# Side rows dealt out by a plan, a third row buffer, and ScalarE fetching in all edge passes of a graph network kernel

## The reference, cut to what matters

```python
h = relu(layernorm(x)); x = x + L0(h)      # typed attention, softmax over each node's incoming edges
h = relu(layernorm(x)); x = x + L1(h)      # gated attention: softmax sum, maximum and mean over edges
h = relu(layernorm(x)); x = x + L2(h)      # polynomial of edge weights, summed per node
h = relu(layernorm(x)); x = x + L3(h)      # three convolutions:
def conv(h, W, b):
    m = concatenate([h[dst], h[src], edge_attr], axis=1) @ W + b
    return segment_sum(m, dst, num_segments=n_nodes)
```

## Time and profile before

| | us |
|---|---|
| profiled execution, time | 11757.73 |
| its span | 11755.6 |
| median of three runs | 11757.57 |
| POOL busy | 8127.3 (69%) |
| VectorE busy | 4012.2 (34%) |
| ScalarE busy | 3490.3 (30%) |
| TensorE busy | 1335.8 (11%) |

### The profile page before, as it was taken

How to read it: one execution, slowest core, us unless ns; L and a number is a source line. 1 busy time by engine, 2 the same in 40 slices (tenths; PEclk the granted TensorE clock), 3 DMA queues, 4 the chain that set the end, 5 groups by cost and what they waited for, 6 DMA issues and landing times. The chain is left out here.

```text
span 11755.6 us, 88443 instructions
## 1 busy us (share of the span) xinstructions
PE 1335.8 (11%) x6735; PEld 1000.0 (9%) x6735; DVE 4012.2 (34%) x5478; ACT 3490.3 (30%) x4561; POOL 8127.3 (69%) x8534
## 2 busy tenths in 40 slices
PE   6100000030000000496111000200000010000001
PEld 4100000020000000374000000200000010000001
DVE  3365555645555555696111111111111101111111
ACT  3333333312222222375333222223222212332221
POOL 5777777677777776401777777677777767777776
PEclk8555555555555555798555555555555555555555
DMA  9333333323333333000222222222222212222222
GB/s 348 129 112 108 108 108 111 105 39 102 110 110 107 113 107 81 13 1 23 67 65 66 65 68 62 62 51 56 53 56 56 53 50 51 56 53 56 56 53 50
DMA packets 448676, 922.38 MB, mean 78 GB/s; under 512 B 211206, under 2 KB 241837, under 8 KB 432952
## 3 DMA queue, kind: packets, MB, share of 16 engines
q0 software_dynamic: 272736, 378.88, 14.7%
q1 hardware_dynamic: 157672, 535.74, 12.5%
q10 hardware_dynamic: 17648, 2.29, 0.1%
HBM read 456.45 MB, written 459.77 MB: 78 GB/s over the span
## 5 line engine op out<-in xcount | busy, mean ns | idle before, releaser
L912 POOL DMA_INDIRECT arena<-tab,src x6087 | 5746.2, 944 | 2631.0 <-issue 1890.5
L2334 DVE TENSOR_TENSOR_SCAN arena<-cv_keep,arena 128x768 f32<-128x768 f32 (+1 forms) x476 | 751.9, 1627 | 5040.6 <-ACT arena L2190 5040.6
L912 POOL DMA_INDIRECT arena<-tab,spread x1539 | 1453.1, 944 | 469.3 <-issue 469.0
L2179 ACT COPY cv_keep<-keep 128x736 f32<-128x736 f32 x204 | 166.0, 814 | 2707.6 <-issue 2707.6
L2195 ACT COPY arena<-arena 128x1472 f32<-128x1472 f32 (+1 forms) x204 | 588.2, 2883 | 551.6 <-DVE arena L2334 551.6
L2190 ACT COPY arena<-arena 128x1472 f32<-128x1472 f32 x204 | 545.2, 2673 | 666.4 <-DMA arena<-tab,src 430.0
L1147 PE MATMUL e_t<-ident,arena 128*68 128x128 f32 (+1 forms) x2 | 0.8, 396 | 4037.2 <-PEq L1492 2046.4
L2258 PE MATMUL cv_t<-ident,arena 128*81 128x128 f32 (+1 forms) x294 | 137.9, 469 | 2616.8 <-ACT arena L2202 1722.9
L1147 PEld LDWEIGHTS e_t<-ident,arena 128*68 128x68 f32 (+1 forms) x2 | 0.3, 132 | 4037.6 <-issue 4037.6
L2272 PE MATMUL cv_t<-ident,arena 128*64 128x128 f32 (+1 forms) x3 | 1.3, 426 | 2975.7 <-ACT arena L2195 2975.7
L1835 PE MATMUL po_u<-arena,Hn 128*128 128x448 bf16 x1564 | 300.9, 354 | 279.9 <-DVE Hn L1942 279.9
(11 more groups left out here) (373 smaller groups left out, 6810.2 us busy)
## 6 DMA issues: line engine op xcount, KB each, us to landing
arena<-tab SPq DMA_DIRECT2D x11520, 0.2 KB
arena<-tab ACTq DMA_DIRECT2D x6912, 0.2 KB
rows<-arena SPq DMA_DIRECT2D x68, 1506.5 KB, 5.6
rows3b<-arena SPq DMA_DIRECT2D x136, 736.0 KB
arena<-tab,src POOLq DMA_INDIRECT x6087
rows<-arena SPq DMA_DIRECT2D x68, 920.0 KB
rows<-arena SPq DMA_DIRECT2D x68, 828.0 KB, 4.5
arena<-tab SPq DMA_DIRECT2D x3200, 0.5 KB
```

What stands on the lines that cost most here:

```text
L912: pool.indirect_dma_start(out=rows[b][:, j, :], out_offset=None, in_=table, in_offset=bass.IndirectOffsetOnAxis(ap=idx[:, at:at + 1].bitca ...
L2334: ins = v.tensor_tensor_scan(out=part, data0=keep[:, 0:(f1 - f0) * C1], data1=part, initial=0.0, op0=ALU.mult, op1=ALU.add)
```

## The change

A function `rows_plan` deals the pieces of all side columns to the iterations of the loop over blocks, evenly: a piece goes to iteration i at the latest where its block is i - closes, at the earliest where it is i - opens, and in between by its share of all pieces. SP and ScalarE each have their plan in every pass; ScalarE's part (pieces 5 to 7) comes at the end of its loop body, for block c + 2. Each piece waits for its buffer on its own. Attention and gated attention have side columns in 3 of 4 blocks, the second and third convolution in 13 of 16; the convolutions have three row buffers.

```diff
-ATT_SHARE = (2, 5)
-CONV_SHARE = (3, 4)
-SP_ROWS = 80
+ATT_SHARE = (3, 4)
+GATED_SHARE = (3, 4)
+CONV_SHARE = ((3, 4), (13, 16), (13, 16))
+SP_EDGE = 80
+SP_CONV = 80
+def rows_plan(share, first, stop, opens, closes):
+    jobs = [(c, k) for c in range(LISTED) if aided(c, share) for k in range(first // LOADS, stop // LOADS)]
+    plan = [[] for _ in range(NC)]
+    at = 0
+    for i in range(NC):
+        while at < len(jobs) and (jobs[at][0] + closes <= i or
+                                  jobs[at][0] + opens <= i and at * LISTED < (i + 1) * len(jobs)):
+            plan[i].append(jobs[at])
+            at += 1
+    return plan
...
@@ attention_edges_phase
+        of_sp = rows_plan(ATT_SHARE, 0, SP_EDGE, -1, 0)
+        of_act = rows_plan(ATT_SHARE, SP_EDGE, P, -3, -2)
...
-                for later in (0, 1):
-                    if aided(c + later, ATT_SHARE):
-                        wait(sp, s_wtd, c + later - 2)
-                        chunks = range(0, P // LOADS // 2) if later else range(P // LOADS // 2 if c else 0, P // LOADS)
-                        fetch_rows(nc, sp, mybir.EngineType.SP, g.lists[:, 0, :], g.tab0, c + later, chunks,
-                                   kvr[(c + later) % 3], s_side[side_of(c + later, ATT_SHARE)[0]])
+                for x, k in of_sp[c]:
+                    wait(sp, s_wtd, x - 2)
+                    side_rows(sp, mybir.EngineType.SP, x, k)
...
                 nc.scalar.copy(out[:, :, 0:D].rearrange("p j f -> p f j"), mix[:, :, 1:C1]).then_inc(s_copied, 1)
+                for x, k in of_act[c]:
+                    wait(act, s_wtd, x - 2)
+                    side_rows(act, mybir.EngineType.Activation, x, k)
...
@@ gated_edges_phase
+        of_sp = rows_plan(GATED_SHARE, 0, SP_EDGE, -2, -1)
+        of_act = rows_plan(GATED_SHARE, SP_EDGE, P, -3, -2)
...
                 nc.scalar.copy(out[:, :, 0:D].rearrange("p j f -> p f j"), mix[:, :, 1:C1]).then_inc(s_copied, 1)
+                for x, k in of_act[c]:
+                    wait(act, s_wtd, x - 2)
+                    side_rows(act, mybir.EngineType.Activation, x, k)
...
@@ conv_layer
-    for b in range(2):
+    for b in range(3):
         rin[b], at = view(g, at, C, D)
...
+        of_sp = rows_plan(share, 0, SP_CONV, -3, -2)
+        of_act = rows_plan(share, SP_CONV, P, -3, -2)
+        def side_rows(eng, engine, c, k):
+            wait(eng, s_in, c - 2)
+            fetch_rows(nc, eng, engine, g.lists[:, 2, :], g.tab3, c, range(k, k + 1), rin[c % 3],
+                       s_side[side_of(c, share)[0]])
...
             for c in range(NC):
-                wait(sp, s_in, c + 1)
-                if k == 0 and c + 2 < NC:
+                wait(sp, s_in, c + 1 if c else 0)
+                if k == 0 and c + 2 < NC and c:
                     load_attrs(c + 2)
-                side_rows(sp, mybir.EngineType.SP, c + 2, early)
+                half = (len(of_sp[c]) + 1) // 2 if c else len(of_sp[c])
+                for x, part in of_sp[c][:half]:
+                    side_rows(sp, mybir.EngineType.SP, x, part)
...
                 wait(sp, s_copied, c + 1)
                 sp.dma_start(dest[:, c * C:c * C + C, :], rows).then_inc(s_st, 16)
-                side_rows(sp, mybir.EngineType.SP, c + 2, late)
+                for x, part in of_sp[c][half:]:
+                    side_rows(sp, mybir.EngineType.SP, x, part)
...
                 give(c)
-                if len(of_act):
-                    act.wait_ge(s_in, c + 1)
-                    side_rows(act, mybir.EngineType.Activation, c + 2, of_act)
+                if c:
+                    for x, part in of_act[c]:
+                        side_rows(act, mybir.EngineType.Activation, x, part)
```

More of the change, by code:

```diff
@@ L960, in attention_edges_phase @@
         works = work[:, :].rearrange("p (f j) -> p f j", j=C1)
+        of_sp = rows_plan(ATT_SHARE, 0, SP_EDGE, -1, 0)
+        of_act = rows_plan(ATT_SHARE, SP_EDGE, P, -3, -2)
+        def side_rows(eng, engine, c, k):
+            fetch_rows(nc, eng, engine, g.lists[:, 0, :], g.tab0, c, range(k, k + 1), kvr[c % 3],
+                       s_side[side_of(c, ATT_SHARE)[0]])
         @block.gpsimd
@@ L1496, in gated_edges_phase, with side_rows @@
         pre, prob = few[:, 0, :], few[:, 1, :]
+        of_sp = rows_plan(GATED_SHARE, 0, SP_EDGE, -2, -1)
+        of_act = rows_plan(GATED_SHARE, SP_EDGE, P, -3, -2)
+        def side_rows(eng, engine, c, k):
+            fetch_rows(nc, eng, engine, g.lists[:, 1, :], g.tab1, c, range(k, k + 1), rin[c % 3],
+                       s_side[side_of(c, GATED_SHARE)[0]])
         @block.gpsimd
@@ L1502, in _ @@
                 .then_inc(s_first, 16)
-            gather_columns(pool, g.tab1, g.src, rin, s_gath, s_wtd, ATT_SHARE)
+            gather_columns(pool, g.tab1, g.src, rin, s_gath, s_wtd, GATED_SHARE)
         @block.sync
@@ L1565, in _ @@
                 dve.wait_ge(s_flags, c + 1)
-                dve.wait_ge(s_gath[c % 3], gathered(c, ATT_SHARE, 3))
-                if aided(c, ATT_SHARE):
-                    slot, full = side_of(c, ATT_SHARE)
+                dve.wait_ge(s_gath[c % 3], gathered(c, GATED_SHARE, 3))
+                if aided(c, GATED_SHARE):
+                    slot, full = side_of(c, GATED_SHARE)
                     dve.wait_ge(s_side[slot], full)
@@ L2051, in conv_layer @@
     s_ea = [sem(f"attrs{b}") for b in range(2)]
-    s_gath = [pool_sem(g, f"gathered{b}") for b in range(2)]
+    s_gath = [pool_sem(g, f"gathered{b}") for b in range(3)]
     s_side = [sem(f"side{n}") for n in range(4)]
+    share = CONV_SHARE[k]
     s_row = pool_sem(g, "fixed_rows")
@@ L2064, in conv_layer @@
     at = 0
-    rin, ea, hd = ([None] * 2 for _ in range(3))
-    for b in range(2):
+    rin = [None] * 3
+    ea, hd = ([None] * 2 for _ in range(2))
+    for b in range(3):
         rin[b], at = view(g, at, C, D)
@@ L2094, in conv_layer, with side_rows @@
         block = inner.enter_context(nc.Block())
[L2096 to L2100, removed]
+        of_sp = rows_plan(share, 0, SP_CONV, -3, -2)
+        of_act = rows_plan(share, SP_CONV, P, -3, -2)
+        def side_rows(eng, engine, c, k):
+            wait(eng, s_in, c - 2)
+            fetch_rows(nc, eng, engine, g.lists[:, 2, :], g.tab3, c, range(k, k + 1), rin[c % 3],
+                       s_side[side_of(c, share)[0]])
         @block.gpsimd
         def _(pool):
-            gather_columns(pool, g.tab3, g.src, rin, s_gath, s_in, CONV_SHARE)
+            gather_columns(pool, g.tab3, g.src, rin, s_gath, s_in, share)
             fix = bass.IndirectOffsetOnAxis(ap=g.fix[:, 0:1].bitcast(U32), axis=0)
@@ L2138, in _ @@
                     load_attrs(c)
-            early, late = range(0, SP_ROWS // LOADS // 2), range(SP_ROWS // LOADS // 2, SP_ROWS // LOADS)
-            for c in range(2):
-                side_rows(sp, mybir.EngineType.SP, c, range(0, SP_ROWS // LOADS))
             for c in range(NC):
-                wait(sp, s_in, c + 1)
-                if k == 0 and c + 2 < NC:
+                wait(sp, s_in, c + 1 if c else 0)
+                if k == 0 and c + 2 < NC and c:
                     load_attrs(c + 2)
-                side_rows(sp, mybir.EngineType.SP, c + 2, early)
+                half = (len(of_sp[c]) + 1) // 2 if c else len(of_sp[c])
+                for x, part in of_sp[c][:half]:
+                    side_rows(sp, mybir.EngineType.SP, x, part)
+                if k == 0 and not c:
+                    wait(sp, s_in, 1)
+                    load_attrs(2)
                 wait(sp, s_copied, c + 1)
                 sp.dma_start(dest[:, c * C:c * C + C, :], rows).then_inc(s_st, 16)
-                side_rows(sp, mybir.EngineType.SP, c + 2, late)
+                for x, part in of_sp[c][half:]:
+                    side_rows(sp, mybir.EngineType.SP, x, part)
             n_out = 0
@@ L2182, in take @@
                     act.wait_ge(s_chained, c)
-                act.wait_ge(s_gath[b], gathered(c, CONV_SHARE, 2))
-                if aided(c, CONV_SHARE):
-                    slot, full = side_of(c, CONV_SHARE)
+                act.wait_ge(s_gath[c % 3], gathered(c, share, 3))
+                if aided(c, share):
+                    slot, full = side_of(c, share)
                     act.wait_ge(s_side[slot], full)
@@ L2189, in take @@
                     nc.scalar.copy(chain[:, D:R3, 1:C1], ea[b].rearrange("p j f -> p f j"))
-                nc.scalar.copy(chain[:, 0:D, 1:C1], rin[b].rearrange("p j f -> p f j")).then_inc(s_in, 1)
+                nc.scalar.copy(chain[:, 0:D, 1:C1], rin[c % 3].rearrange("p j f -> p f j")).then_inc(s_in, 1)
             def give(c):
@@ L2214, in copy_z @@
                 nc.scalar.copy(z[:, t, :], ps_o[b][:, 0:D]).then_inc(s_z, 1)
-            of_act = range(SP_ROWS // LOADS, P // LOADS)
             scale(0)
-            for c in range(2):
-                side_rows(act, mybir.EngineType.Activation, c, of_act)
+            for x, part in of_act[0]:
```

(1 more changed line is left out.)

## The result

The changed kernel takes 12370.68 us (median of 4 runs, 12369.15 to 12383.37) against 11758.11 us for the kernel before (4 runs): ratio 1.052, 95% interval 1.0502 to 1.0538. The forecast was 12,390 (12,280 to 12,500). The profiled execution took 12383.37 us, its span is 12381.6, which is 626 us more than before.

What follows compares the result with a forecast made beforehand. POOL's gathers bound the passes, a buffer besides in the first convolution. Attention +84, gated +557, first convolution -47, second and third together +36 make +630 us on 11757.73: 12,390 us, range 12,280 to 12,500.

Steps and rivals of the forecast that it cites:

- Gathers as the bound: All five edge passes of the kernel before: bound by POOL's number of gathers, 1.25 us each.
- the gated chain: Gated pass: fetch, mask and VectorE's work follow serially, so a block with a fetch takes 41.9 us against POOL's 27.5.
- The price of a fetch: ScalarE's loop end: 18.8 us idle after a 2.8 us copy, 19.0 us more than without a fetch.
- the gated term: Gated pass, first gather to last result copy: 2499 us against 1942.0 before, +557.
- that term: Attention, first gather to last exponentials: ScalarE's chain becomes the limit, 2015 us against 1930.9 before, +84.
- rival B: First two passes: the fetch is covered and POOL stays the bound, 11,644 us in total; chance 0.05.
- SP in the second and third convolution: SP becomes the limit at 35.73 us a block with a side column: +18 us a pass, +36 in all.
- 11 none (9 us): Second and third convolution: 11 of SP's iterations deal no column and take 9 us together.
- the forecast's signs: Second and third convolution of the changed kernel: POOL's waits near the end only, SP without pause.
- Third buffer: First convolution: POOL runs two blocks ahead of the take, covered by SP's dealing, 46.6 us saved.
- C: Half of the fetch runs beside the block's work: gated 32.4 us a block, near 11,840 us in total; chance 0.04.
- D: SP's dealing dominates the convolutions at 37.1 us a column: 12,530 us in total; chance 0.04.

Runs made afterwards that it cites:

- e2: Changed kernel with ScalarE filling the gated pass's next mask and weights before its fetch instead of after: 12189.61 us, ratio 1.0365 to the kernel before.
- e5: Changed kernel with side columns in 3/4 instead of 13/16 of the blocks in the second and third convolution: 12235.22 us, ratio 1.0389 to the kernel before.
- e6: Changed kernel with SP dealing each block's rows one block earlier in all convolutions: 12861.13 us, ratio 1.092 to the kernel before.
- e10: Changed kernel with a fourth row buffer and SP dealing one block earlier, second and third convolution only: 12604.76 us, ratio 1.0719 to the kernel before.
- b1: Kernel before, with the changed kernel's convolutions but side columns in 11/16, 3/4 and 3/4 of their blocks: 11674.46 us, ratio 0.9927 to the kernel before.
- e7: e2, with gated ScalarE pieces dealt 2, 2, 2, 3, one behind the exponentials, up to three blocks ahead, SP's a block earlier: 12169.85 us, ratio 1.0335.
- e9: e7, with SP's gated pieces levelled to 4, 4, 4, 3 for 5, 5, 5, 0 and its lead back to one or two blocks: 11874.17 us, ratio 1.0097.

## Why the prediction was right, step by step

**Gathers as the bound, and the gated chain: right.** The saved gathers bought nothing in the first two passes, since these followed ScalarE. In the gated timeline of the changed kernel every link named in the forecast is there: fetch, mask, VectorE, and POOL waiting for the weighting.

```profile
4010.94 0.35 ACT L1562 COPY arena<-arena 128x64 f32<-128x64 f32 x1 [9.55 <-DVE arena L1640]
...
4012.24 1.80 ACTq L915 DMA_DIRECT2D arena<-tab  x5
4014.00 2.77 ACT L1565 COPY arena<-arena 128x1472 f32<-128x1472 f32 x1
4014.13 19.84 ACTq L915 DMA_DIRECT2D arena<-tab  x43
4034.01 0.78 ACT L1553 COPY ge_pen<-pen 128x736 f32<-128x736 f32 x1 [17.24 <-issue]
...
4034.93 0.20 DVE L1600 TENSOR_TENSOR arena<-arena,ge_small 128x23 f32<-128x23 f32 x1 [23.82 <-ACT ge_small L1554]
...
4047.78 0.95 POOL L926 DMA_INDIRECT arena<-tab,src  x1 [8.42 <-DVE arena L1632]
```

**The price of a fetch: mis-sized, 17.4 for 19.0 us.** From L1562 to the next mask are 4034.01 - 4010.94 = 23.07 us; without a fetch 5.63. I took the price from the convolutions, where the fetch starts 1.3 us after a copy that has just waited. Here too it starts 1.3 us after such a copy (L1562), but two large copies (L1564, L1565) are then still to run, and the first starts go out beside them. So the interval with a fetch is 40.4 us in the mean, not 41.9, and the one without 23.1, not 22.9: 46 x 1.46 - 20 x 0.2 = 63 us of the 67 by which the gated term was too high. In attention the fetch starts together with the last copy. The timeline shows a long interval, 32.85 us from exponentials to exponentials; the mean of the 46 is 32.1, not 32.9, and 46 x 0.88 - 20 x 0.14 = 38 us are what that term was too high by.

```profile
1120.16 0.25 ACT L1025 ACTIVATE ae_prob<-arena 128x92 f32<-128x92 f32 x1 [6.57 <-DVE arena L1099]
...
1131.47 2.83 ACT L1035 COPY arena<-arena 128x1472 f32<-128x1472 f32 x1
1131.47 21.50 ACTq L915 DMA_DIRECT2D arena<-tab  x48
1153.01 0.25 ACT L1025 ACTIVATE ae_prob<-arena 128x92 f32<-128x92 f32 x1 [18.71 <-issue]
```

The Trainium skill (Advanced Engine Details and Errata, Sequencer Loop) says that engine instructions are pushed into a queue, where they wait for their semaphores, and that the sequencer goes on to read the next. That the starts begin under queued copies agrees (4012.24, before L1565 at 4014.00). That they begin only behind the copy that waits (4010.94) suggests that the reading ahead ended at that wait; no run shows why.

The rule behind rival B, that starting is usually small beside the transfer (the Trainium skill, DMA: Bandwidth & Descriptors, Issuing engines are not separate DMA queues), does not carry over to a whole fetch of single rows: in e2 SP's 80 starts take 32.35 us, and VectorE goes on with the rows 1.6 us after them.

**SP in the second and third convolution: mis-sized, +57 for +18.** The failed step is "11 none (9 us)", a turn of SP without pieces taken at 0.8 us. Turns with pieces measure 35.9 us (10570.96 to the next store at 10606.90), as forecast from the earlier trace rows. But the timeline of the changed kernel (SP and ScalarE's take and give, third convolution) at an empty turn:

```profile
10531.71 0.38 SPq L2184 DMA_DIRECT2D rows3b<-arena  x1
10534.81 11.99 SPq L915 DMA_DIRECT2D arena<-tab  x32
10535.09 2.68 ACT L2232 COPY arena<-arena 128x1472 f32<-128x1472 f32 x1 [8.60 <-DMA rows3b<-arena]
10546.90 0.37 SPq L2184 DMA_DIRECT2D rows3b<-arena  x1
10547.92 2.67 ACT L2227 COPY arena<-arena 128x1472 f32<-128x1472 f32 x1 [9.18 <-DMA arena<-tab]
10551.86 19.05 SPq L915 DMA_DIRECT2D arena<-tab  x48
...
10570.96 0.37 SPq L2184 DMA_DIRECT2D rows3b<-arena  x1
```

The two turns take 39.25 us, not 36.5. SP stands from 10547.27 to 10551.86: it waits for the take (10547.92), which waits for the rows that SP has just started. I had let SP run on from one column to the next. Eleven such pairs, 39.1 to 40.2 us in the second convolution, make some 34 of the 39 us that were missing. Two of the forecast's signs failed with it: SP does pause, and POOL's waits for the take begin in the middle of these passes, not near their end. That SP's pace is the limit at 13/16 is shown by e5, and ScalarE, which fetches too, waits there for SP's store (8.60 us before its give at 10535.09); that the missing part is this stall is read from the trace only, since e6 and e10 failed to take it away.

The price of an empty turn could have been read before the change. The second convolution of the kernel before has the same stall (SP, and ScalarE's take): two turns in 39.55 us, 3.8 more than one with pieces and not 0.8, with SP standing from 8190.71 to 8195.24.

```profile
8168.37 0.38 SPq L2148 DMA_DIRECT2D rows3b<-arena  x1
...
8190.34 0.37 SPq L2148 DMA_DIRECT2D rows3b<-arena  x1
...
8191.29 2.67 ACT L2190 COPY arena<-arena 128x1472 f32<-128x1472 f32 x1 [14.73 <-DMA arena<-tab]
...
8195.24 12.63 SPq L901 DMA_DIRECT2D arena<-tab  x32
8207.92 0.37 SPq L2148 DMA_DIRECT2D rows3b<-arena  x1
```

**Third buffer: right in kind, -30 for -47.** The same mistake: I gave SP 113 us for four blocks (three of 37.1 and under 2) and so a cover of 27 us; its empty turns cost more here too (41.3 us or more with the turn beside them, for 39), four blocks take 116 to 117 us, and POOL still waits 32.7 us for the take. With 11/16 in b1 this pass takes 1897.2 us, 56 less than before, with no wait for a consumer. No run has the new dealing with two buffers, so which of the two brings the gain isn't shown.

**What went right by luck.** Attention and gated were too high by 105 us, the convolutions too low by 94, so the sum is nearer than its terms. The range of 110 us to either side also isn't the sum of the bounds given with it, which is -71 and +246. Of the rivals, B falls by POOL's 513.8 us of waits in the gated pass, C (32.4 us a block) by the 40.4 us, D by the 35.9 us of a turn, though the empty turns cost a good part of what D expected (+57 of its +87 a pass). In the gated pass the forecast named the right limit, but not what stood behind it. The mask's place behind the fetch is worth 195 us alone (e2). With ScalarE out of the way SP's five pieces a block still hold the pass at 2190 us (e7), where the forecast had them fit in without a cost. And e9 has the same fetches on the same engines and none of the loss.

## What to carry to other kernels

Where an engine both computes and starts many small transfers, the place of the starts in its program mattered more here than their number: put first what another engine waits for, and deal the starts in pieces that fit each block's idle time (the gated pass went from 2399 to 1896 us with nothing but their order and dealing changed). A queue at the limit doesn't catch up in a pause in which it waits for its own last delivery, so size it by whole periods read from store to store. Whether two queues that feed the same buffers should pause in the same block is worth a run; e6 and e10 only suggest it. Prefer the share that leaves the feeder some slack: 11/16 beat 3/4 in the first convolution (1897 against 1924 us), and 3/4 beat 13/16 in the others (1895 against 1964).

## What the hardware showed unexpectedly

Copies that ran beside the DMA starts of the same engine did not slow the starts themselves. In the changed kernel the 16 starts of a piece on ScalarE's queue take 5.4 to 5.7 us in the median, in attention and the second convolution and also beside two large copies in the gated pass. What is longer there is the pause before the second piece, where its offsets are loaded: 4.0 us in the median, against 1.45 before the third piece and before either in the second convolution. So the 48 starts take 21.7 us there (4012.24 to 4033.97), and 19.55 us where only the end of one copy lies beside them. The row is longer too in the gated pass (520 bytes for 256), but the third piece shows no trace of that; why the one pause grows stays open.

And SP's first rows behind a store start late: its queue shows them 2.8 to 3.5 us after the store's start in the second and third convolution (10531.71 to 10534.81) where it goes on without a wait, and 3.3 to 4.3 us in the gated pass. What takes the time isn't shown.
